# Four-head value product moved ahead of the interleaved score and row matmuls in an attention pipeline

## The reference

```
scores = q @ k.T / sqrt(d)         # 256 x 256, per head
scores = mask(scores)              # stages 0, 1, 3: causal; stages 2, 4: none
probs  = softmax(scores)
out    = probs @ v                 # then @ Wo, added to x
```

## The kernel before, in words

| step | m mod 4 | besides the weave |
|---|---|---|
| A | 1 | values; ScalarE copies OB behind its exponentials |
| B | 2 | none |
| C | 3 | values, waits for that copy (even k) |
| D | 0 | turn_sums; VectorE's division |

## Time and profile before

### The profile page before, as it was taken

How to read it: one execution, slowest core, us unless ns; L and a number is a source line. 1 busy time by engine, 2 the same in 40 slices (tenths; PEclk the granted TensorE clock), 3 DMA queues, 4 the chain that set the end, 5 groups by cost and what they waited for, 6 DMA issues and landing times. The chain is left out here.

```text
span 1408.4 us, 30563 instructions
## 1 busy us (share of the span) xinstructions
PE 1127.7 (80%) x10377; PEld 540.0 (38%) x10377; DVE 910.1 (65%) x1742; ACT 788.3 (56%) x1471; POOL 554.4 (39%) x611
## 2 busy tenths in 40 slices
PE   3678676887299999998587769999778867786997
PEld 1344453545234444433222343333344533234333
DVE  4668647786666677766689634455568758973454
ACT  2257412674155555554278547888537734883786
POOL 2115102451145555555025227877501201211686
PEclk7779868798599999999779969999979987997899
DMA  6721004110054444442711013323151013100422
GB/s 197 266 93 55 2 0 152 33 34 2 7 139 132 126 125 130 126 132 68 242 32 32 2 40 89 92 90 90 58 176 49 18 62 106 47 3 5 102 90 75
DMA packets 106524, 116.96 MB, mean 83 GB/s; under 512 B 16195, under 2 KB 75787, under 8 KB 105379
## 3 DMA queue, kind: packets, MB, share of 16 engines
q1 hardware_dynamic: 104116, 102.07, 24.7%
q10 hardware_dynamic: 2288, 13.31, 2.6%
HBM read 96.21 MB, written 18.79 MB: 82 GB/s over the span
## 5 line engine op out<-in xcount | busy, mean ns | idle before, releaser
L1295 POOL TENSOR_TENSOR work<-Ks,work 128x512 f16<-128x512 f32 x308 | 356.4, 1157 | 236.9 <-ACT work L1374 228.9
L727 ACT ACTIVATE work<-ps 128x384 f32<-128x384 f32 (+1 forms) x640 | 304.1, 533 | 173.1 <-PE ps L583 106.9
L826 DVE TENSOR_REDUCE bmax<-ps 128x6 f32<-128x768 f32 (+1 forms) x320 | 335.5, 1056 | 69.5 <-PE ps L561 48.4
L1308 PE MATMUL ps<-ao,wf 128*128 128x512 f16 x1320 | 340.5, 384 | 13.8 <-DVEq L1395 6.6
L1418 DVE TENSOR_TENSOR Ks<-ps,Qs 128x512 f32<-128x512 f32 x304 | 210.0, 691 | 151.8 <-ACT ps L1366 123.4
L1324 PE MATMUL ps<-work,wf 128*128 128x512 f16 x924 | 253.8, 384 | 4.7 <-POOL work L1295 3.6
L1308 PEld LDWEIGHTS ps<-ao,wf 128*128 (+1 forms) x1320 | 119.9, 99 | 190.3 <-issue 55.0
L1374 ACT CAST work<-Ks 128x512 f16<-128x512 f32 x308 | 187.7, 610 | 3.8 <-DVE Ks L1418 3.5
L864 POOL TENSOR_SCALAR mx<-bmax 128x16 f16<-128x16 f32 x80 | 24.9, 311 | 377.7 <-DVE bmax L832 218.8
L572 PE MATMUL ps<-Qs,Ks 32*128 32x256 f16 x640 | 124.3, 296 | 56.2 <-issue 19.2
L605 PE MATMUL ps<-work,V 128*9 128x256 f32 (+1 forms) x2560 | 160.3, 371 | 0.0
(11 more groups left out here) (166 smaller groups left out, 1399.6 us busy)
## 6 DMA issues: line engine op xcount, KB each, us to landing
Qs<-scrC SPq DMA_DIRECT2D x256, 128.0 KB, 3.0
Qs<-scrC SPq DMA_DIRECT2D x88, 256.0 KB, 3.1
Qs<-scrQ SPq DMA_DIRECT2D x40, 256.0 KB, 3.1
Ks<-scrK SPq DMA_DIRECT2D x40, 256.0 KB, 3.3
scrK<-work SPq DMA_DIRECT2D x60, 128.0 KB, 2.2
scrQ<-work SPq DMA_DIRECT2D x60, 128.0 KB, 2.6
Qs<-mxT SPq DMA_DIRECT2D x320, 1.0 KB
wf<-in_L_w ACTq DMA_DIRECT2D x2, 1792.0 KB, 9.4
```

What stands on the lines that cost most here:

```text
L727: act.activation(prob[:, g % 8, 0:W1], ps[:, 4 + g % 3, 0:W1], ACT.Exp, scale=float(att["dk"]) ** -0.5).then_inc(exped, 1)
L826: dve.tensor_reduce(bmax[:, n // 4 % 2, 2 * (n % 4):2 * (n % 4) + 2, 0:NB], ps[:, b0:b0 + 2, 0:W1].rearrange("p i (n w) -> p i n w", n=NB) ...
L1295: pool.tensor_tensor(hparts[:, (m + r) % 4, 1, :], weighted(m + r), hparts[:, (m + r) % 4, 0, :], ALU.subtract).then_inc(second, 1)
L1308: ins = pe.matmul(out, weight_parts(which, wpart, j), xh[:, xpart, c * CH:(c + 1) * CH], start=(i == 0), stop=(i == 2))
```

## The change

The call of `values` is moved within the step. It stood behind the weave; it now stands behind the waits at the head of the step and ahead of the weave. No instruction, buffer or wait is added or taken away.

```diff
--- before.py
+++ after.py
@@ -658,6 +658,8 @@
                         pe.wait_ge(max_in[m // 4 % 2], 64 * (m // 8 + 1))
                     if m >= 2:
                         pe.wait_ge(exped, 2 * m - 2)
+                if m >= 3 and m % 2 == 1 and (m - 3) // 2 < NPAIR // 2:
+                    values((m - 3) // 2)
                 for j in range(PIECES + SKEW):
                     if j == SKEW and 1 <= m < NPAIR:
                         pe.wait_ge(exped, 2 * m - 1)
@@ -671,8 +673,6 @@
                     project_values(n)
                 elif NC < n < LEAD:
                     keep_warm(n)
-                if m >= 3 and m % 2 == 1 and (m - 3) // 2 < NPAIR // 2:
-                    values((m - 3) // 2)
                 for u in range(NUNIT):
                     if n == turn_step(u):
                         turn_sums(u)
```

## The result

The changed kernel took 1475.5 us (median of four runs, 1469.95 to 1481.61) against 1397.4 us of the kernel before (1394.82 to 1402.14): a ratio of 1.0556, with a 95% interval of 1.0503 to 1.0609, or some 78 us. Forecast were 1466 us and +70, with a range of 1448 to 1484. The profiled execution after has a span of 1471.7 us. Two executions of the experiments, 1447 us of c_front and 1492 us of after_again, were over 1.5% above the fastest of their kernel and are left out of the ratios; the first is the only trace of c_front, so only its turns at full clock are read.

The account below looks back on a forecast made before the run. Bound: VectorE in unmasked loops, a circle through ScalarE with no engine full in causal ones. 33.0 causal + 30.2 unmasked + 1.2 + 2.5 + 3.5 gave 70.4 us, 1395.8 to 1466.2 us; range 1448 to 1484.

Parts of the forecast that it names:

- The release stays in front of the product: Head of step A: values still follow VectorE's release, so the product cannot start earlier than the weave starts today.
- Step A: First of a turn's four steps: values ahead of the weave delay it by 0.77 us causal, 0.98 us unmasked.
- Step C waits for the copy: Third step of a turn: the product's wait for the copy of OB becomes binding, with the weave queued behind it.
- today's walk: Causal turn in the old order, summed by the same method: 5.21 us against 5.23.
- rival B: Attention turns: the wait for the copy does not bind; +0.53 causal, +0.98 unmasked, 1440 us in all; chance 0.16.
- The walk of a turn: Terms along one attention turn: 6.23 us causal against 5.23 (+1.00), 7.22 unmasked against 5.78 (+1.44).
- exponentials to copy: Walk term from the start of A's exponentials to the copy of OB: 0.91 us causal, 1.10 unmasked.
- Rival C: Attention loops: the clock falls back inside them, half of the 55 turns at half clock; 1523 us; chance 0.08.
- One change of tiling fewer: Tensor engine, each turn: one tile-shape change less, at most 0.43 x 55 = 24 us gained; not expected on the path.
- The tail: n from 64: D's weave waits for C's exponential, no longer covered by values; 0.7 us a stage, 3.5 in all.
- the one at half clock: One unmasked turn of 22 at half clock: 8.14 us becomes 9.34, +1.2.
- The start of the loops: n = 14 to 18, before any division: +0.3 us a causal stage, +0.8 an unmasked one, 2.5 in all.

Follow-up runs that it names:

- c_front: Against the kernel before, only step C's value product (even k) moved in front of its weave, the other left behind; ratio 1.0248.
- after_again: The changed kernel once more, unaltered, for a second trace; ratio 1.0524 against the kernel before.
- a_front: Against the kernel before, only step A's value product (odd k) moved in front of its weave, the other left behind; ratio 1.0255.
- early_a: Kernel before, causal stages only: step A's product ahead of the waits at the step's head, copy of OB ahead of A's exponentials; ratio 0.9991.
- copy_first: Changed kernel with ScalarE's copy of OB ahead of step A's exponentials instead of behind; 1458 us, ratio 1.0432 against the kernel before.
- after_turn_twice: Changed kernel with step D's four transposes issued twice in the unmasked stages, same data and place; ratio 1.0539 against the kernel before.
- tail_behind: Changed kernel with the product behind the scores again for n of 64 and more; ratio 1.0505 against the kernel before.

## Why the prediction was right

**The release stays in front of the product: right.** In a_front the product stands between release and weave and costs 0.62 us a causal turn; in early_a it stands ahead of the release and costs nothing that can be told.

**Step A, +0.77 and +0.98: right in kind, too dear.** A alone costs 0.62 in causal turns and 0.84 in unmasked ones. In causal turns the product itself takes the 0.77 that was forecast; but today's way from the exponentials to the copy, 0.91, falls to 0.76 once the product stands in front (290.29 to 291.05 in a_front), and 0.77 - 0.15 = 0.62.

**Step C waits for the copy: right.** There are 60 waits of the product for L704, 32.3 us in all. In c_front, where C's product also stands in front, the rows show why it costs only 0.20: against today's walk the product starts 0.69 us sooner behind the copy (0.73 us instead of 0.49 + 0.55 + 0.38), but C's reduction, hidden today, comes onto the path with some 0.93. This step decided between the forecast and rival B (5.8 and 6.8 us a turn), and the turns of 6.04 and 7.03 lie between the two, nearer to the forecast.

**The walk of a turn: right, with three terms off.** Causal, forecast against trace: product 0.77 / 0.77, to the exponentials 0.51 / 0.50, to the copy 0.91 / 0.76, copy and signal 0.65 / 0.73, product 0.77 / 0.77, to the reduction 0.58 / 0.58, two reductions and release 2.04 / 1.95; together 6.23 / 6.06. Unmasked, in the same order and from the turn at 780.30: 0.98 / 0.99, 0.43 / 0.42, 1.10 / 0.97, 0.65 / 0.74, 0.98 / 0.98, 0.51 / 0.50, 2.57 / 2.46; together 7.22 / 7.06. VectorE was to be idle some 1.5 us a turn, released by L561 or L556; it is 1.30 causal and 1.01 + 0.54 = 1.55 unmasked in the turns shown. The term "exponentials to copy" was mis-sized: the 0.91 of the earlier trace rows was not set by ScalarE's work, which needs 0.76, but by A's product, for which the copy waits and which then ended last (287.27 to 288.25 is 0.98, as good as the 0.97 from product to copy in copy_first). With the product in front, the copy follows the exponentials at once.

**Half clock inside the loops: the part that was missing.** Rival C, at 8%, had the clock falling back inside the loops, as a case that would replace the forecast, with half of all turns. It came as an addition: 9 to 12 us in the two traces, in unmasked loops only. The argument against it, a window of 30% busy at full clock, was weak: one quiet window right behind steady work says little about a loop that repeats its quiet stretch. The Trainium skill, TensorE: Matmul & The Clock Gate, in its section on a second HAM failure mode (HAM is its name for the unit that sets this clock), says of another kernel that micro-idles between groups of matmuls make the clock oscillate. The trace agrees in kind: between groups the engine is idle for up to 0.67 us (0.66 ahead of C's product at 783.42), and the clock goes between 1.00 and 0.50. But after_turn_twice has idle stretches as long, up to 0.67 us, at a clock of 1.00, so they alone do not decide.

**One change of tiling fewer: no effect.** The Trainium skill, TensorEngine Tiling (Array Packing), Key Properties, says that changing the tiling mode drains the engine; by an estimate with it the change could have cost up to 24 us less. Nothing of it shows: the seven terms of either walk add up to the whole turn, and the product in front still takes 0.77 and 0.98 to 0.99 from its start to the weave's.

**The tail: mis-sized.** 0.7 us a stage was forecast and 1.5 to 2.0 came, 9 us in all; by tail_behind 1.2 to 1.8 of each come from the product's place.

**The sum**, by the first trace: 33 causal turns x 0.82 = 27 (forecast 33.0), 21 unmasked x 1.25 = 26 (30.2), falls 9 (0), tails 9 (3.5), the rest of the first turns, the one at half clock among them, about 1 (1.2). That is 72 from the first reciprocal of each stage to its last. The start of the loops, forecast at 2.5, lies ahead of the first reciprocal: from the first reduction to the first reciprocal the five stages take 163 us before and after in this pair of traces, and 158 and 163 in the second, so the term can't be told from the clock's scatter. The forecast of 70.4 was too dear in the turns and too cheap in clock and tails, and the two cancelled; that the total came out so near is in part luck. The 78 us of the timed runs agree with both within their interval (70 to 85 us).

**Left open:** what the wait for the copy costs by itself; why work added in step C's hole does not hold the clock when work in D does, by its place or by its kind; some 10 us of c_front; and whether the falls cost in timed runs what they cost in traces.

## What to carry to other kernels

An instruction between a wait and the work that others wait for can cost its whole length, since all of them get their work that much later: here 0.62 us a turn for a product of 0.77. The same instruction in front of the wait cost next to nothing (turns of 5.16 us against 5.23), and behind the work that others wait for it was hidden in the kernel before. When a block is moved earlier in its step, look which waits it doesn't pass, and walk one period with it between release and the work released. Look too whether its own second wait, met for free until now, becomes the last: here the wait for a copy that had always been on time.

## What the runs showed of the hardware that was not expected

The granted clock fell from 1.00 to 0.50 inside a loop in which the tensor engine is busy 63% of the time on average (21.99 of 35.00 us) and never idle for more than some 0.7 us at a stretch. The causal loops with the same order, busy 73% (48.64 of 66.36 us in stage 1), never fell once the clock had risen. With 0.5 us more of matmul work a turn, in the stretch right ahead of where the falls begin, the clock stayed up (50.73 of 73.00 us busy, 69%); with a like amount of other work in another place, at the same 69%, it did not. The average busy share alone does not tell.
